# Layer norms of later token tiles between the stages of a QKV block, and finer waits ahead of the output projection

## The reference, cut to what matters

```python
x = x + attn(layernorm(x))     # x: 4 x 2048 x 2048; 32 heads of 64, 8 kv heads
x = x + ffn(layernorm(x))      # I = 8192

def attn(x):
    q = x @ Wq + bq            # 2048 -> 2048
    k = x @ Wk + bk            # 2048 -> 512
    v = x @ Wv + bv            # 2048 -> 512
    p = softmax(q k^T / 8)     # each kv head serves 4 q heads
    return (p @ v) @ Wo + bo

def ffn(h):                    # weights are integers 0..255, (w - 128) * scale of the row
    return (silu(h @ Wg^T) * (h @ Wu^T)) @ Wd^T
```

## Time and profile before

| | |
|---|---|
| median of 2 runs | 2751.28 us (2746.69 and 2755.86) |
| profiled execution, time | 2750.0 us |
| span of its slowest core (core 2) | 2748.4 us |
| spans of the cores | 2697.7 to 2748.4 us |
| PE, DVE, ACT busy | 82%, 29%, 25% of the span |
| Phase A ends, phase B ends, phase C ends | about 425, 1014 and 1162 us |

### The profile page before, as it was taken

The page is one execution under the profiler, slowest core; times in us unless marked ns, Lnnn a source line. Parts: engine busy times, 40 slices in busy tenths (PEclk is TensorE's granted clock), DMA queues, the critical chain, the costliest instruction groups (busy, mean ns, idle before and its releaser), DMA issues.

```text
span 2748.4 us, 27169 instructions; the slowest of 8 cores (2697.7 to 2748.4 us)
## 1 busy us (share of the span) xinstructions
PE 2246.3 (82%) x10458; PEld 933.5 (34%) x10624; DVE 803.6 (29%) x923; ACT 680.9 (25%) x714; POOL 223.1 (8%) x233
## 2 busy tenths in 40 slices
PE   0676778888888866917997998989989999899995
PEld 0333332222222212413443443434434444344442
DVE  5535441222221212372050140320501403205017
ACT  2101006888888850021101101001011010010110
POOL 1020100000000000010101101011011010110100
PEclk9997988988998887957999999999999999999998
DMA  9292901000000035174929739578297384781932
GB/s 189 65 121 64 105 16 28 17 17 17 13 16 17 17 64 128 62 105 39 77 24 101 69 52 87 46 92 70 23 115 69 54 86 45 92 77 16 117 36 123
DMA packets 366108, 176.73 MB, mean 64 GB/s; under 512 B 342912, under 2 KB 347136, under 8 KB 361632
## 3 DMA queue, kind: packets, MB, share of 16 engines
q0 software_dynamic: 345680, 130.04, 45.0%
q1 hardware_dynamic: 20304, 44.95, 4.9%
HBM read 296.33 MB, written 8.65 MB: 111 GB/s over the span
## 4 chain that ended last, share of the span: by engine, by line
PE 74%; DMA 11%; DVE 9%; issue 4%; ACT 1%; DVEq 0%; SPq 0%; ACTq 0%; POOLq 0%
PE PS_C L205 22%; PE PS_A L205 20%; PE PS_B L205 19%; PE PS_D L205 11%; DMA arena<-uwt 5%; DVE st L246 4%; DVE arena L246 4%; DMA arena<-wq 3%; DVE rrow L246 2%; DMA arena<-xt 1%; PE PS_D L216 1%; PE PS_B L201 1%; PE PS_A L201 1%; ACT arena L233 1%; PE PS_D L201 1%
## 5 line engine op out<-in xcount | busy, mean ns | idle before, releaser
L205 PE MATMUL PS_A<-arena 128*128 128x512 bf16 (+1 forms) x2710 | 683.3, 395 | 135.3 <-DVE arena L246 69.4
L205 PE MATMUL PS_C<-arena 128*128 128x512 bf16 (+1 forms) x2345 | 675.5, 401 | 102.5 <-DVE rrow L246 81.1
L205 PE MATMUL PS_B<-arena 128*128 128x512 bf16 (+1 forms) x2471 | 600.0, 383 | 5.8 <-ACT arena L233 1.8
L205 PEld LDWEIGHTS PS_A<-arena 128*128 128x128 bf16 (+1 forms) x2763 | 274.4, 100 | 547.7 <-issue 266.6
L205 PEld LDWEIGHTS PS_B<-arena 128*128 128x128 bf16 (+1 forms) x2519 | 245.9, 98 | 359.7 <-issue 83.9
L246 DVE TENSOR_TENSOR arena<-arena 128x1024 bf16<-128x1024 bf16 (+2 forms) x112 | 85.6, 764 | 934.6 <-ACT arena L233 932.9
L205 PE MATMUL PS_D<-arena 128*128 128x512 bf16 (+1 forms) x1230 | 325.3, 385 | 2.8 <-ACT arena L233 1.4
L205 PEld LDWEIGHTS PS_C<-arena 128*128 128x128 bf16 (+1 forms) x2380 | 179.3, 105 | 350.0 <-issue 238.8
L233 ACT ACTIVATE arena<-PS_A,gs2b 128x1024 bf16<-128x1024 f32 x64 | 71.3, 1113 | 882.2 <-PE PS_A L201 882.2
L216 PE MATMUL PS_D<-identb,arena 128*128 128x128 bf16 x336 | 41.9, 306 | 226.9 <-DVE arena L246 226.7
L233 ACT ACTIVATE arena<-PS_A 128x1024 bf16<-128x1024 f32 x171 | 185.4, 1084 | 97.6 <-PE PS_A L201 97.6
(11 more groups left out here) (51 smaller groups left out, 940.2 us busy)
## 6 DMA issues: line engine op xcount, KB each, us to landing
arena<-gwt POOLq DMA_DIRECT2D x64, 512.0 KB, 8.8
arena<-uwt POOLq DMA_DIRECT2D x64, 512.0 KB, 8.9
arena<-dwt POOLq DMA_DIRECT2D x64, 512.0 KB, 18.1
arena<-xt SPq DMA_DIRECT2D x24, 1024.0 KB, 5.6
arena<-wq POOLq DMA_DIRECT2D x32, 512.0 KB, 12.3
arena<-scr_r SPq DMA_DIRECT2D x64, 128.0 KB
out<-arena SPq DMA_DIRECT2D x8, 1024.0 KB, 4.0
arena<-wo POOLq DMA_DIRECT2D x1, 4096.0 KB, 30.9
```

The costliest lines, as they stand in the source:

```text
L205: e.matmul(o, ll, rr, start=a, stop=b, tile_position=t))
```

## The change

Two things are rearranged; no arithmetic changes.

In phase A `qkv_block` gets a list of tiles whose norms it emits between its own stages: one after the four K groups, one after the four V groups, one after the copy-out of Q group 7 and one at its end. Block 0 takes tiles 8 to 11, block 1 takes tiles 12 to 15. The norms after the blocks are gone; the transposes stay where they were.

In phase C the first token tile no longer waits for all 32 units' normalisation before its first matmul. `norm_bydc` gives for each dc the last normalisation that writes to it, and ahead of the matmuls of each dc of tile 0 PE waits for that one. The wait for the copy-out of unit 31 (`dve_ctev[31]`) moves ahead of tile 1, the first to write `PS_C`. SP loads x for tile 0 after the context matmuls of unit 31, and for tile 1 still after the normalisation of unit 31.

```diff
-        def qkv_block(blk):
+        def qkv_block(blk, bg=()):
+            bg = list(bg)
+
+            def bg_step():
+                if bg:
+                    ln_compute(bg.pop(0))
...
                     bk2b[:, miq:miq + 1], inc=True)
+            bg_step()
...
                     bvbb.rearrange("p (k n) -> p k n", k=8), inc=True)
+            bg_step()
...
                             inc=(hh == 1))
+                    if miq == 7:
+                        bg_step()
+            while bg:
+                bg_step()
             pe_qkv_end[blk] = C['pe']
...
-        qkv_block(0)
-        for g in range(8, 12):
-            ln_compute(g)
+        qkv_block(0, bg=(8, 9, 10, 11))
         for g in range(8, 12):
             tr_tile(g)
-        qkv_block(1)
-        for g in range(12, 16):
-            ln_compute(g)
+        qkv_block(1, bg=(12, 13, 14, 15))
...
+        norm_bydc = {}
+        for uu in range(32):
+            _, pju = units[uu]
+            for hh_ in _heads_of_pair(pju):
+                dcu = hh_ // 2
+                norm_bydc[dcu] = max(norm_bydc.get(dcu, 0), dve_norm[uu])
...
         t_wait(ACT, act_exp[(31, 15)])
-        t_wait(DVE, dve_ctev[31])
-        t_wait(DVE, dve_norm[31])
         for tm in range(8):
-            if tm < 2:
+            if tm == 0:
+                y_wait(PE, pe_ctx[31])
+            if tm == 1:
                 y_wait(DVE, dve_norm[31])
...
+            if tm == 1:
+                t_wait(DVE, dve_ctev[31])
             for dc in range(16):
-                if tm == 0 and dc == 3:
-                    t_wait("WWO2", wd_wo_mid)
-                if tm == 0 and dc == 11:
-                    t_wait("WWO3", wd_wo_late)
+                if tm == 0:
+                    t_wait(DVE, norm_bydc[dc])
+                    if dc == 3:
+                        t_wait("WWO2", wd_wo_mid)
+                    if dc == 11:
+                        t_wait("WWO3", wd_wo_late)
```

## The result

| | before | changed |
|---|---|---|
| median of all runs, us | 2765.13 (10 runs) | 2708.38 (11 runs) |
| ratio to before, 95% interval | | 0.9804, 0.9769 to 0.9840 |
| the same once more, on another chip (`e1_changed`) | | 0.9834, 0.9801 to 0.9867 |
| profiled execution, span of the slowest core | 2748.4 | 2702.4 |

The forecast was 2709 us and a gain of 1.5%. The two series give 2.0% and 1.7%, 54 and 46 us of 2765; the two profiled executions differ by 46 us.

The account below looks back on a forecast made before the run. Layer norms on DVE were taken to set the phase A gaps, transfers the wait ahead of the projection, DMA the Q stage's pace. -47.0 + 5 + 12 - 10.9 = -40.9 us from 2750.0 gave 2709 us, range 2694 to 2728.

Parts of the forecast that it names:

- The gaps: Phase A, behind blocks 0 and 1: each gap loses all but one layer norm on DVE, together -47.0 us.
- The stops of PE: Q stages: moved norms delay Q copies, stopping PE 3.4 and up to 4.2 us per block; 15.2 at most, +5 taken.
- I take 0 net: Q stages: stops may drop PE's clock, 2.9 us each, but slow groups let loads catch up; 0 net, up to 8.7.
- The x loads: Q stages: three 1 MB loads now fall beside the Wq stream and hold it back, 4 us each, +12 us.
- Their sum: Q stages of both blocks: stops +5 and x loads +12 us, against -47.0 in the gaps, giving -30.0 for phase A.
- The projection: Output projection: part of tile 0's matmuls run before the last normalising multiply, so tile 1 starts 10.9 us earlier.
- The four start times: Projection tile 0: 12 matmuls right behind phase B, then groups about 20, 35 and 43 us later.
- 1 (swallowed): Q stages: stops and loads both fall into existing waits; gain 59.5 us, 2690; chance 0.10 for it or most of it.
- 2 (paid in full): Q stages: stops, loads and slow groups add up; gain 16.6 us, 2733; chance 0.18 for it or most of it.
- 4: Output projection: tile 0 waits for a later third Wo load, so nothing is gained there; 2720; chance 0.05.
- 5: Both Q stages: the clock stays low, 32 groups at 2.9 us more, 93 us; slower than before, 2785; chance 0.04.
- 3: Q stages: the norm's operation on DVE holds up POOL's Wq descriptors, up to 1.35 us each, 5.4 us; 2715; chance 0.15.

Follow-up runs that it names:

- e5_small_x: Changed kernel with the x loads of tiles 11, 12 and 15 cut to 32 of 2048 columns; blocks 0 and 1 together took 193.8 us.
- e3_waits_only: Kernel before with only the finer waits ahead of the output projection, phase A as before; ratio to before 0.9963 (0.9940 to 0.9986).
- e7_small_wq: Changed kernel with all Wq loads but the first four cut to one chunk of 128 rows; blocks 0 and 1 together took 187.5 us.

## Why the prediction was right, point by point

- **The gaps.** Predicted -47.0, measured -46.6 (40.2 + 39.7 to 16.9 + 16.4). A count of one norm's length, and it held to half a us.
- **The stops of PE.** Their length was right: 3.2 us in the rows and 15.0 us of four in all, against 3.4 and 15.2. The term taken for them, +5, was too small: they cost 9.2 (`e5_small_x`). The prediction had 10.2 us of 15.2 hidden in the waits for Wq. They hid 12.5, but of 21.7: "I take 0 net" for the clock left out 6.7 us. In the changed kernel's timeline on core 3, the group at 257.27 took 4.77 us and the one at 284.10 5.00 in place of 3.40, behind 3.22 and 2.69 us idle.
- **The x loads.** The term of +12, 4 us each, was too large: 2.2 each by themselves and 1.2 to 2.8 for all three beside the stops. The DMA share over 1 was read as "no room", but at the same share 134 GB/s went through in place of 108. The prediction named an x load that costs much less than 3 us as a sign of being wrong, and larger waits for Wq as a sign of being right; by both, this step failed.
- **Their sum.** The blocks grew by 11.4 to 12.0 us against 17. One term was 4 us short and the other 9 to 11 over, so the sum was 5 to 6 over. That 2709 was hit within 1 us is luck: the sum took 40.9 us from 2750.0, and the first series measured 2708.38 at a ratio of 0.9804, which is 54 us from about 2762. A starting point 12 us too low and a gain 13 us too small cancelled.
- **The projection.** Predicted -10.9 at tile 1, measured 58.7 to 47.0 between the two slowest cores (-11.7), -12.8 in the mean over the cores and -10 in the timed ratio of `e3_waits_only`. The four start times of 0, 20, 35 and 43 us were met by 0, 20, 33 and 42. That the wait would stay and only matmuls move was right (43.2 to 41.9 us). What the prediction did not see is that the last wait is the edit's own and no need of tile 0's data.
- **The rivals.** 1 (swallowed) and 2 (paid in full) both fell: 12 us lie between 0 and the 41 of the upper bounds, nearer the lower. 4 fell, as the third Wo load landed 9 us before the last multiply. 5 fell: slow groups appear, but singly. 3 was partly there: the timeline of POOL in the changed kernel, with the normalising operation of DVE at 139.40 for 1.34 us, shows

```profile
139.79 1.71 POOL L172 DMA_DIRECT2D arena<-wq  x1 [2.46 <-PE PS_A L201]
146.48 1.14 POOL L172 DMA_DIRECT2D arena<-wq  x1 [4.98 <-PE PS_A L201]
...
254.59 1.87 POOL L172 DMA_DIRECT2D arena<-wq  x1 [2.30 <-PE PS_A L201]
```

  All issues of the Q stage of block 0 took 1.14 or 1.15 us before; those that start under a normalising operation take 1.71 to 1.87. Each of the three in this trace (139.79, 254.59 and 289.88, of 1.81 us) ends 0.76 or 0.77 us after the normalising operation over it does. The delay is 0.6 to 0.7 us each, 2.0 us in all. Only the slice issued at 139.79 was waited for, 0.55 us ahead of group 5; the ring hid the rest. The Trainium skill (SBUF — State Buffer, "A bandwidth-pool intuition that's wrong (but worth ruling out)") describes this lock; the trace agrees that it exists and puts its price here at half of what the prediction gave it.

## What to carry to other kernels

Work moved in front of copies that a matmul stage waits for is paid for by the length of each piece against the slack of that copy: pieces of up to 3.5 us, about the time of one group, did not stop PE here, and a piece of 7.9 us cost a stop of up to 4.4 us and often the slow clock after it. Two causes of waiting in one stage with a ring of buffers in it did not add here, so measure each with the other taken away before giving them prices. Where small transfers stand in a chain next to a large load, the load can make most of the chain's length. And count a wait from the columns that are read, not from the buffer they lie in.

## What the runs showed of the hardware that was not expected

- A stop of 3.2 us on PE sometimes brings the clock down and sometimes doesn't: in the changed kernel the group after 3.22 us idle took 3.40 us at 142.31 and 4.77 at 257.27; in `e7_small_wq` it took 6.28 after 3.23. Over the cores of `e7_small_wq` a slow group followed 8 of 16 such stops, and all 16 of 4.3 us.
- Three x loads of 1 MB in the stream of Wq loads of the Q stages lengthened the blocks by 2.2 us each (6.5 in all, with an error of 2), more through slow groups (4.4) than through later slices (2.7).
- A transfer of 4 KB from DRAM took 10.0 us to be seen beside a Wo load and 1.6 us without it.
